# A selective scan behind a gated convolution, on one core: the depthwise convolution in three steps over four column groups, and the end of the layer norm on TensorE

## What is computed

```python
y = jax.vmap(dw)(xs, agg_w)                      # 3x3 depthwise, weights of this image
y1 = jnp.einsum('bchw,oc->bohw', y, b1_w) + b1_b[None, :, None, None]
y2 = jnp.einsum('bchw,oc->bohw', y, b2_w) + b2_b[None, :, None, None]
g = jax.nn.gelu(y1, approximate=False) * y2
mu = g.mean(axis=1, keepdims=True)
var = g.var(axis=1, keepdims=True)
gn = (g - mu) / jnp.sqrt(var + LN_EPS)
x1 = x + gn * ln_w[None, :, None, None] + ln_b[None, :, None, None]
...
def step(h, inp):                                # over the 4096 pixels of an image
    dt_t, B_t, C_t, x_t = inp
    h = jnp.exp(dt_t[..., None] * A) * h + dt_t[..., None] * B_t[:, None, :] * x_t[..., None]
    return (h, jnp.einsum('bdn,bn->bd', h, C_t))
...
x = jax.nn.silu(_group_norm(x, gn_gamma, gn_beta)) + x1
```

## Time and profile before

| | |
|---|---|
| median of 3 runs | 14144.98 us (14141.27 to 14147.53) |
| the profiled execution | 14140.41 us |
| its span, first to last instruction | 14138.6 us |
| granted TensorE clock, mean | 0.873 |
| busy share | DVE 96%, POOL 94%, ACT 86%, PE 79% |
| span / 256 chunks | 55.2 us |

### The profile page before, as it was taken

How to read it: one execution, slowest core, us unless ns; L and a number is a source line. 1 busy time by engine, 2 the same in 40 slices (tenths; PEclk the granted TensorE clock), 3 DMA queues, 4 the chain that set the end, 5 groups by cost and what they waited for, 6 DMA issues and landing times.

```text
span 14138.6 us, 163967 instructions
## 1 busy us (share of the span) xinstructions
PE 11234.8 (79%) x33024; PEld 3336.7 (24%) x33024; DVE 13504.3 (96%) x12083; ACT 12099.3 (86%) x24489; POOL 13256.0 (94%) x3076
## 2 busy tenths in 40 slices
PE   7778878788787878778777878777787877887787
PEld 2222222222222222222222222222222222222221
DVE  7999999999999999999999999999999999999999
ACT  7888888888888888888888888888888888888888
POOL 6999999999999999999999999999999999999999
PEclk9888888888888888888888888888888888888887
DMA  5556565556656565556566565655656565656554
GB/s 132 141 138 142 140 149 136 143 137 145 144 141 144 136 146 140 144 139 142 140 146 145 137 146 135 149 138 142 143 138 145 142 144 137 144 140 147 140 140 117
DMA packets 1068261, 1992.06 MB, mean 141 GB/s; under 512 B 123649, under 2 KB 124730, under 8 KB 1067066
## 3 DMA queue, kind: packets, MB, share of 16 engines
q1 hardware_dynamic: 1065786, 1979.41, 58.7%
q10 hardware_dynamic: 1280, 0.02, 0.0%
HBM read 1626.62 MB, written 352.32 MB: 140 GB/s over the span
## 4 chain that ended last, share of the span: by engine, by line
POOL 62%; issue 35%; DVE 1%; ACT 1%; PE 1%; POOLq 0%; ACTq 0%; DMA 0%; SPq 0%; DVEq 0%
POOL hq L973 44%; POOL dbx L965 18%; DVE hq L861 0%; ACT ps_a L592 0%; POOLq L963 0%; ACTq L504 0%; DVE dbx L844 0%; POOLq L972 0%; PE pp L325 0%; PE ps_acc L417 0%; ACT dbx L606 0%; PE pp L361 0%; PE ps_b L405 0%; PE pp L376 0%; DVE pp L820 0%
## 5 line engine op out<-in xcount | busy, mean ns | idle before, releaser
L973 POOL TENSOR_TENSOR hq<-hq,c_rep 128x2048 f32<-128x2048 f32 x2048 | 9264.5, 4537 | 772.6 <-ACT carry L611 767.7
L861 DVE TENSOR_TENSOR_SCAN hq<-ps_a,dbx 128x512 f32<-128x512 f32 x8192 | 9438.2, 1203 | 132.7 <-ACT dbx L606 75.2
L592 ACT ACTIVATE ps_a<-dt_rep,A_neg 128x512 f32<-128x512 f32 x8192 | 5626.1, 687 | 1416.8 <-DVE hq L861 1354.7
L965 POOL TENSOR_TENSOR dbx<-dtx_rep,b_rep 128x2048 f32<-128x2048 f32 (+1 forms) x1024 | 4082.4, 3987 | 88.5 <-DMA dtx_rep<-dtx_d 88.5
L606 ACT ACTIVATE dbx<-ps_a,dbx,carry 128x1 f32<-128x1 f32 x7168 | 2505.5, 350 | 225.8 <-POOL dbx L965 124.2
L844 DVE TENSOR_TENSOR dbx<-dtx_rep,ps_b 128x2048 f32<-128x2048 f32 (+1 forms) x1280 | 2622.9, 2049 | 4.1 <-PE ps_b L405 4.1
L417 PE MATMUL ps_acc<-hq,dsum 128*32 128x512 f32 x16384 | 2339.2, 645 | 166.7 <-POOL hq L973 166.6
L325 PE MATMUL pp<-xin,diag 128*128 128x504 f32 (+3 forms) x4608 | 2212.8, 608 | 6.0 <-ACT diag L637 6.0
L405 PE MATMUL ps_b<-dbl,bsel 41*128 41x512 f32 x2560 | 1481.5, 659 | 465.5 <-DVE dbx L844 289.4
L361 PE MATMUL pp<-x,W_taps 128*128 128x512 f32 x768 | 685.4, 990 | 976.3 <-DVE x L815 630.8
L325 PEld LDWEIGHTS pp<-xin,diag 128*128 128x128 f32 x4608 | 792.8, 189 | 1397.8 <-issue 1397.8
(11 more groups left out here) (117 smaller groups left out, 9990.2 us busy)
## 6 DMA issues: line engine op xcount, KB each, us to landing
dtx_rep<-dtx_d SPq DMA_DIRECT2D x2048, 256.0 KB, 5.5
dt_rep<-dt_d SPq DMA_DIRECT2D x2048, 256.0 KB, 5.7
c_rep<-bc_d SPq DMA_DIRECT2D x1024, 256.0 KB, 5.4
b_rep<-bc_d SPq DMA_DIRECT2D x1024, 128.0 KB, 2.9
dtx_d<-sp SPq DMA_DIRECT2D x256, 512.0 KB, 2.8
dt_d<-dt SPq DMA_DIRECT2D x256, 512.0 KB, 6.0
out<-o SPq DMA_DIRECT2D x128, 512.0 KB, 3.6
xin<-in_x SPq DMA_DIRECT2D x192, 320.0 KB, 8.5
```

Source lines behind the costliest of these rows:

```text
L592: A(ps_a[:, BANK[i], :], dt_rep[:, q // NQ, g, :], ACT.Exp, scale=A_neg[:, q // NQ, q % NQ, g:g + 1]).then_inc(exp_done, 1)
L861: v.tensor_tensor_scan(hq[:, q % HQ, g, :], ps_a[:, BANK[i], :], dbx[:, slot(q), g, :], 0.0, ALU.mult, ALU.add).then_inc(scan_done, 1)
L965: g.tensor_tensor(dbx[:, slot(q), m:, :], dtx_rep[:, d, m:, :], b_rep[:, c % 2, q % NQ // 2, :].unsqueeze(1).to_broadcast([P, DG - m, T]), ...
L973: g.tensor_tensor(quad, quad, c_rep[:, c % 2, q % NQ, :].unsqueeze(1).to_broadcast([P, DG, T]), ALU.mult).then_inc(cmul_done, 1)
```

## The change

The convolution no longer moves 128 channels for each of nine taps. The image rows are loaded three times, shifted by one row each, into `xr`: 96 partitions are 3 shifts by 32 channels, and the 128 channels lie in four groups side by side. One matmul with K = 96 sums three taps of a column of the 3x3 window for 32 channels, and the four groups write four column groups. So a chunk has 3 steps of 4 matmuls (96 x 32) in place of 9 matmuls (128 x 128). SyncE gets three more loads per chunk (`load_shifted`, 256 KB each), and `xin` loses its halo rows. `zero_rows` on ScalarE clears the row outside the image, for two chunks of eight. The weights are prepared with `mask_taps`, `spread_taps`, `keep_taps` and a new `make_diag` (12 activations of 96x32); attention and weights move one chunk ahead (attention to c = 4, weights to steps 24 to 31 of c = 5).

The layer norm's end: `rstd` leaves 1/sqrt(var) in PSUM (`pp[:, 2, :]`) in place of SBUF. VectorE multiplies the gate `gbuf` by it (`scale_gate`, after scan 30, a chunk's second last). TensorE then makes x1 in PSUM with two matmuls at step 31: `cw`, which is the centring matrix with ln_w in it, times the scaled gate, and the identity times `xin`. ScalarE adds ln_b and writes x1 (`evac_x1`, step 0 of the next chunk). `norm` and `add_input` are gone.

Further: y_gate of the last chunk's second half stands after scan 9 in place of scan 8, behind the shared `weigh_inputs`. `b_rep` and one half of `sz` have one buffer in place of two; the loads of `b_rep` are split in two parts, each behind a wait for GpSimd's last read.

```diff
-PE_CONV = (8, 9, 11, 12, 13, 14, 15, 16, 17)
+PE_CONV = (11, 12, 13)
+PE_X1, ACT_X1 = 31, 0
-DVE_NORM, DVE_Y1, DVE_DT, DVE_Y0, DVE_GATE = 0, 8, 16, 24, 23
+DVE_NORM, DVE_Y1, DVE_DT, DVE_Y0, DVE_GATE = 30, 9, 16, 24, 23
-POOL_CHUNKS, POOL_SLOTS, ATT_CHUNK = (1, 2, 3, 4), (10, 11), CH - 3
+POOL_CHUNKS, POOL_SLOTS, ATT_CHUNK = (1, 2, 3, 4), (10, 11), CH - 4
+TAP_SPREAD, TAP_MM, TAP_KEEP, TAP_DIAG = 24, 26, 28, (30, 31)
...
+            def load_shifted(b, c):
+                if not (isinstance(b, int) and b * CH + c == 0):
+                    sp_e.wait_ge(conv_done, b * CH + c)
+                    sp_e.sem_inc(wait_taken, 1)
+                img = x_d[bass.ds(b + c // CH, 1), :, :]
+                r0 = ROWS * (c % CH) - 1
+                for j in range(3):
+                    ra, rb = max(r0 + j, 0), min(r0 + j + ROWS, H)
+                    sp_e.dma_start(xr[DW * j:DW * j + DW, :, (ra - r0 - j) * W:(rb - r0 - j) * W],
+                                   img[:, :, ra * W:rb * W].rearrange("o (g c) l -> (o c) g l", g=GROUPS)
+                                   ).then_inc(xr_loaded, 16)
...
+                ca, cb = (1 if kw == 0 else 0), (W - 1 if kw == 2 else W)
+                for g in range(GROUPS):
+                    acc = pp[DW * g:DW * g + DW, 2, :].rearrange("p (r w) -> p r w", w=W)
+                    rows = xr[:, g, :].rearrange("p (r w) -> p r w", w=W)
+                    last = mm(acc[:, :, ca:cb], diag[:, kw, g, :], rows[:, :, ca + kw - 1:cb + kw - 1],
+                              start=(kw == 1), stop=(kw == 2), skip_group_check=True)
...
+            def step_x1(b, c):
+                pe.wait_ge(scaled, b * CH + c + 1)
+                mm(pp[:, 2, :], cw[:], gbuf[:], start=True, stop=False)
+                mm(pp[:, 2, :], w["ident"][:], xin[:, c % 2, :], start=False, stop=True).then_inc(x1_mm, 1)
...
-                A(sq[:], sq[:], ACT.Exp, scale=-0.5).then_inc(rstd_done, 1)
+                A(pp[:, 2, :], sq[:], ACT.Exp, scale=-0.5).then_inc(rstd_done, 1)
+
+            def evac_x1(b, c):
+                act.wait_ge(x1_mm, b * CH + c + 1)
+                if c % CH == 2 and not (isinstance(b, int) and b * CH + c < CH):
+                    act.wait_ge(fin_done, CH * b)
+                A(x1_cols(c), pp[:, 2, :], ACT.Identity, bias=w["vec0"][:, 3:4]).then_inc(x1_done, 1)
...
-            def make_diag(b):
-                act.wait_ge(att_done, b + 1)
-                for k in range(TAPS):
-                    last = A(diag[:, k, :], w["ident"][:], ACT.Identity, scale=wts[:, k:k + 1])
...
+                for kw in ((0, 1), (2,))[k]:
+                    for g in range(GROUPS):
+                        last = A(diag[:, kw, g, :], dsum[0:96, :], ACT.Identity, scale=wsel[:, g, kw:kw + 1])
...
-            def norm(b, c):
+            def scale_gate(b, c):
                 dve.wait_ge(rstd_done, b * CH + c + 1)
-                v.scalar_tensor_tensor(pp[:, 2, :], pp[:, 2, :], w["vec0"][:, 2:3], sq[:], ALU.mult, ALU.mult).then_inc(t2_done, 1)
-
-            def add_input(b, c):
-                dve.wait_ge(t2_done, b * CH + c + 1)
-                v.scalar_tensor_tensor(x1_cols(c), pp[:, 2, :], w["vec0"][:, 3:4],
-                                       xin[:, c % 2, W:W + T], ALU.add, ALU.add).then_inc(x1_done, 1)
+                v.tensor_tensor(gbuf[:], pp[:, 2, :], gbuf[:], ALU.mult).then_inc(scaled, 1)
```

163 lines of the change are left out of this document (115 added, 48 removed).

## The result

The change makes the kernel slower. The median is 14500.8 us (14490.0 to 14509.8, 4 runs) against 14146.3 us for the kernel before in the same comparison: a ratio of 1.025, with the interval 1.0235 to 1.0266. The prediction had said 14028 us. The sign was wrong, and the time lies above the range.

The account below looks back on a forecast made before the run. VectorE (96%) and GpSimd (94%) were taken as the bound. Plain chunks at -0.93 us and per-image extras gave -3.5 us an image, by 32 images -112 us from 14140.4: 14028 us, range 13860 to 14270.

Parts of the forecast that it names:

- pays nothing itself: Convolution on TensorE: 3.4 us less work per chunk, x1 included, gains nothing itself apart from an earlier dt product.
- busy from S-1.1 on: Chunk turn, S being scan 0's start: TensorE works on x1, select and xh from S-1.1; xh ends at S+7.8.
- scan 9 at S+14.2: Plain chunk: scan 9 starts 14.2 us after scan 0's start S, in place of 16.2.
- rival D: Convolution: the four groups do not overlap, TensorE gets 9.5 us per chunk more, 14300 us or above; chance 0.02.
- the forecast's circle: Plain chunk: the VectorE and ScalarE circle of waits, 14.2 + 36.75 + 0.87 = 51.8 us.
- Rival A: Chunk turn: TensorE is cold when x1 is wanted, chunk +1.9 us, kernel 14170 to 14620 us; chance 0.18.
- A's break-even: End of xh: at S+9.4 nothing is gained (scan 9 at S+15.3); each microsecond beyond costs one.
- 36.75 + 0.87: Plain chunk from scan 9 to its end: 36.75 us as before, plus 0.87 for y_gate, scale_gate and the vanished softplus wait.
- The plain chunk at 52.0: Plain chunk: 51.8 us by the circle, with 0.2 of carry waits left standing, 52.0 us, -0.93.
- the +1.5: Chunk of the diagonals and its effect: make_diag's 12 activations load ScalarE, scan 4 about 1.5 us late per image.
- the forecast's extras for the pair: Group norm chunk and the next: +0.67 for scale_gate ahead of residual adds, +0.6 for evac_x1 ahead of keep_first.
- Transfers at nothing: DMA: three shifted loads add 0.7 MB per chunk, 9%, and b_rep's loads wait for GpSimd; all put at no cost.

Follow-up runs that it names:

- e3: The changed kernel with the first convolution step repeated six times more on TensorE, result unchanged: 14137.3 us, 0.9992 of the kernel before.
- e2: The changed kernel with norm and add_input back on VectorE, convolution still in three steps: 14086.8 us, 0.996 of the kernel before.
- e9: The kernel before with only y_gate moved from behind scan 8 to behind scan 9: 14086.6 us, 0.9954.
- e7: e2 with the first convolution step repeated six times more: 13992.1 us, 0.9886 of the kernel before.
- e4: The changed kernel with two unneeded matmuls ahead of x1 in five of eight chunks: 14314.4 us, 1.0131 of the kernel before.
- e5: e3 plus two unneeded matmuls ahead of x1 in five of eight chunks: 14186.3 us, 1.0029 of the kernel before.
- e15: e14 plus two unneeded matmuls ahead of x1 in five of eight chunks: 14266.8 us, 1.0085 of the kernel before.
- e14: e1 with the nine taps at steps 11 to 16, all behind the dt product: 14180.5 us, 1.0022 of the kernel before.
- e1: The changed kernel with the nine taps of before, x1 still made on TensorE and ScalarE: 14359.0 us, 1.0161 of the kernel before.
- e11: The kernel before with y_gate behind scan 9 and its nine taps at steps 11 to 16, behind the dt product: 13978.4 us, 0.9883.
- e12: e3 with three repeats of the convolution step in place of six: 14495.7 us, 1.0249 of the kernel before.

## Why the prediction was wrong, point by point

The prediction had a plain chunk 0.93 us shorter; it is 1.31 us longer. Two steps failed: that the shorter convolution "pays nothing itself", and that TensorE, "busy from S-1.1 on", would bring x1 and xh early enough for scan 9 at S+14.2.

**The convolution "pays nothing itself": this step failed beside x1's move.** The duration was right (3.2 us forecast, 2.76 measured for the three steps; the groups overlap, so rival D is out). The sentence that followed was that TensorE "waits more than it is waited for". It counted removed work as harmless because the engine had room. What it did not ask is what TensorE stands in front of when the work is gone: the output product, which cannot start before ScalarE has written dt. Nine taps had covered that wait but for 0.63 us, and three steps do not. There follow 5.34 us of idleness, half clock for the output product and b1, a wait of 1.23 ahead of the GELU and of 0.91 at scan 24. Filling the hole brought 363 us back, of 355 lost (e3). Of the 1.22 us by which a plain chunk of e3 is shorter, 0.74 lie between scan 9 and the GELU, in the middle itself; 0.50 lie ahead of scan 9, where the clock of the x1 stretch rose from 0.58 to 0.74 as well. The prediction did expect "more such stretches" of half clock, gave them no place, and priced the clock only at x1.

**The two parts compound, so neither can be called the larger.** Without x1's move the sentence held: three steps with the hole take as long as nine taps (e2 14086.8, e9 14086.6). From e7, where the hole is filled and x1 is made on VectorE, to after are 509 us: the hole alone costs 95 of them (e2), x1's move alone 145 (e3), and 269 come only with both. Why both cost more than the sum of each is not shown. In a plain chunk the forecast's circle missed 1.46 us ahead of scan 9 (15.66 against 14.2) and 0.98 behind it (38.60 against 37.62).

**Rival A had the right mechanism in one of two places.** It said that x1 would be cold and scan 9 late. The clock from 1 us ahead of scan 0 on is 0.58, x1 is done at 2.34 in place of 1.0, and xh ends at 9.39 where the forecast said 7.8; A's break-even was 9.4. "TensorE is now busy from S-1.1 on" failed as the argument against A: x1, the select and half of xh, begun behind 2.21 us of idleness, all ran at half clock. But A's size did not come: scan 9 was at 15.66, not 17.2, and still earlier than before. By A's own rule an xh that ends at 9.39 gives 15.3; ScalarE's two waits for z (1.18 and 0.18 us in the chunk above) are not in that rule. That the measured 14501 us lie inside A's times, 14170 to 14620, is in part luck: 0.98 us of the chunk come from behind scan 9, where A had put nothing.

**Scan 9 at S+14.2: only e4 comes near it.** e4 has 14.41. In the others with x1 on TensorE it is 15.0 to 15.8, also in e5 and e15, where the clock is at 1.00 through xh; so a warm xh is not enough for it. Even e3, with the middle mended, starts it at 15.16, 1.0 us behind the forecast. Of that, 0.6 is the start of the silu block, 8.6 in place of 8.0.

**The rest of the chunk, 36.75 + 0.87: nearly right once the middle is warm.** e3 takes 37.88 us from scan 9 to the end and e14 37.90, against 37.62. After takes 38.60. e5 and e15, warm in the middle too, take 38.38 and 38.53, with waits at scans 12 and 16.

**The plain chunk at 52.0 failed by the two together.** It takes 54.26 in after, 53.04 in e3. Most of the saving on VectorE came (51.68 to 51.07 us of work, forecast 50.9) and did not shorten anything: in the mean VectorE works 0.60 us less in a chunk and waits 1.91 us more. Moving x1 to TensorE cost time beside each convolution: 414 us (after against e2), 272 (e1 against e9), 145 (e3 against e7), 202 (e14 against e11). Where the middle is warm and no tap stands ahead of the dt product, 145 to 202 us are left. The second and the fourth pair also differ in the buffers and the split loads of `b_rep`. I have not divided what is left between ScalarE's evac_x1, scale_gate and the clock. That stays open.

**The extras of an image were about right or smaller.** Means over all images: the chunk with the diagonals is 55.04 us and the one behind it 53.91, around the plain 54.27, so the +1.5 is at most 0.8. The attention chunk is 3.3 us longer than a plain one (before 3.4). The group norm chunk and the next are 120.6 us, +3.3 on before, of which the two plain shares of +1.3 are 2.6; the forecast's extras for the pair were +1.3.

**Transfers at nothing: right.** GpSimd shows no wait for b_rep, and the shares of busy DMA are 0.67 and 0.60 in the windows. A kernel without the new loads is slow (e1), one with them is as fast as before (e3), and e7 with them ties with e11 without them.

**The signs named beforehand.** The prediction said it would be wrong "if TensorE's clock is at half through xh", or if VectorE waited for decays or carries in a plain chunk. The second shows in after, and the first for the first half of xh. The hole in the middle was in no list.

**The clock.** The prediction cited the Trainium skill (TensorE: Matmul & The Clock Gate, "Why this matters for your kernels") as speaking against taking work off a TensorE that already waits. The runs agree: 1088 ns per instruction behind the hole and 618 without it. The rule was right for a place that I had not looked at. It does not give the price: e2 has 1070 ns there and loses nothing against e9.

## What to carry to other kernels

Before work is taken off an engine that has room, look up what stands next in its queue, what that waits for, and what clock it will then get. Here nine taps were the cover of a wait, and taking them away gave nothing by itself and cost 142 us beside x1's move. Work that can't be shortened with profit can be moved: the same nine taps behind the dt product, and one sum's reader one scan later, gave 1.2% for two lines. And a stretch made faster can move the idleness to the next wait, as in e5 and e15, so both have to be read after the edit.

## What the runs showed of the hardware

- The loss from an idle TensorE is not in step with its length here: halving the idle time ahead of the output product (1353 us in all in after, 699 in e12) left its instructions at 1005 ns, and only taking nearly all of it away (91 us, e3) brought 618.
- 48 added matmul instructions a chunk, 5.15 us of work on TensorE (2.76 to 7.91), made the kernel 363 us faster than after (e3), and 95 us faster where x1 is made on VectorE (e7 against e2).
- The same cold product stands in two kernels that are 414 us apart: it is at 1088 ns in after and at 1070 in e2.
- Warming one stretch cooled the next: clock 0.58 and 0.98 in after (-1 to 8 and 8 to 22 us), 1.00 and 0.86 in e4; 0.75 and 0.90 in e14, 1.00 and 0.81 in e15.
- Three steps of four matmuls with 96 rows each, in four column groups, took 2.76 us as 24 instructions: 0.92 us a step.
